# Two fused cross-attention layers: the value products of layer 0 in two sets of head groups, the text keys behind all other key pieces

## What is computed

```
# layer 0
q = heads(x @ Wq.T)
out = softmax(q k_text / 4) v_text + softmax(q k_ip / 4) v_ip
x1 = out @ Wo.T + bo + x
# layer 1: 371 text rows, 4 image rows
probs = softmax(q k / 4);  out = probs v
qsem = l2norm(probs @ text)            # compared with the 4 image rows
p_ip = softmax(q k_ip / 4 + 0.5 * qsem . l2norm(ip)) * mask
y = (out + p_ip v_ip) @ W_out + b_out + x1
```

## Time and profile before

| | before |
|---|---|
| median of 3 runs | 2611.76 us |
| profiled execution, its span | 2613.9 us, 2612.1 us |
| TensorE busy | 2475.8 us, 95% |
| VectorE, ScalarE, GpSimd busy | 1637.9, 1232.6, 767.3 us |
| length of a slot (batch 10: 1178.51 to 1256.80) | 78.3 us |

### The profile page before, as it was taken

The page is one execution under the profiler, slowest core; times in us unless marked ns, Lnnn a source line. Parts: engine busy times, 40 slices in busy tenths (PEclk is TensorE's granted clock), DMA queues, the critical chain, the costliest instruction groups (busy, mean ns, idle before and its releaser), DMA issues.

```text
span 2612.1 us, 64042 instructions
## 1 busy us (share of the span) xinstructions
PE 2475.8 (95%) x26280; PEld 2128.5 (81%) x26280; DVE 1637.9 (63%) x3210; ACT 1232.6 (47%) x2305; POOL 767.3 (29%) x999
## 2 busy tenths in 40 slices
PE   6689999999999999999999999999999999999996
PEld 5578888888888888888888888888888888888874
DVE  2246765666765666776666676566676556677655
ACT  2334445544445544445544445544444544444543
POOL 2123323323323323323322332322322322333222
PEclk7799999999999999999999999999999999999997
DMA  7455777556677555677565777655677655567620
GB/s 181 104 97 87 104 103 93 83 92 92 95 103 91 96 89 86 95 100 107 83 90 86 93 110 101 85 88 86 99 96 104 89 86 89 87 94 101 89 38 7
DMA packets 493225, 241.46 MB, mean 92 GB/s; under 512 B 259627, under 2 KB 492923, under 8 KB 492924
## 3 DMA queue, kind: packets, MB, share of 16 engines
q1 hardware_dynamic: 492934, 237.37, 61.2%
HBM read 171.35 MB, written 64.59 MB: 90 GB/s over the span
## 4 chain that ended last, share of the span: by engine, by line
PE 76%; DVE 17%; issue 2%; SPq 2%; DMA 2%; ACT 1%; POOL 0%; DVEq 0%; ACTq 0%; POOLq 0%
PE ST L690 7%; DVE w L827 6%; PE PN L707 5%; PE R L734 5%; PE R L632 4%; PE R L645 4%; PE R L646 4%; DVE m L911 4%; PE R L583 4%; PE R L584 4%; PE PN L752 3%; PE R L648 3%; PE R L791 3%; PE R L586 3%; DVE w L824 3%; PE ST L672 2%
## 5 line engine op out<-in xcount | busy, mean ns | idle before, releaser
L1126 ACT ACTIVATE p<-ST 128x1344 f32<-128x1344 f32 x320 | 413.6, 1293 | 114.6 <-PE ST L693 110.1
L1256 POOL TENSOR_TENSOR w<-w 128x448 f32<-128x448 f32 (+1 forms) x256 | 330.8, 1292 | 426.3 <-DVE w L824 408.2
L827 DVE SCALAR_TENSOR_TENSOR w<-p,pr 128x1344 f32<-128x1344 f32 x160 | 296.7, 1854 | 174.9 <-ACT pr L1141 161.7
L824 DVE TENSOR_TENSOR rem<-R,kst 128x298 f32<-128x298 f32 (+2 forms) x184 | 91.4, 497 | 455.1 <-ACT kst L1024 455.1
L734 PE MATMUL R<-pr,Gh 128*128 128x448 f32 (+1 forms) x960 | 367.6, 383 | 0.0
L824 DVE TENSOR_TENSOR w<-R,w 128x448 f32<-128x448 f32 (+1 forms) x480 | 281.6, 620 | 71.5 <-PE R L739 61.1
L645 PE MATMUL R<-wvh,ch 128*128 128x320 f32 (+3 forms) x896 | 302.8, 338 | 16.3 <-ACT V0t L1024 12.6
L1189 POOL TENSOR_TENSOR kst<-rem,kst 128x298 bf16<-128x298 f32 (+2 forms) x184 | 151.2, 822 | 483.3 <-ACT kst L1024 262.0
L646 PE MATMUL R<-wvh,cl 128*128 128x320 f32 (+3 forms) x896 | 279.7, 312 | 0.0
L690 PE MATMUL ST<-Qs,Ks 100*128 100x112 bf16 (+1 forms) x3520 | 229.6, 214 | 14.7 <-DMA Qs<-ms 7.6
L690 PEld LDWEIGHTS ST<-Qs,Ks 100*128 100x128 bf16 (+1 forms) x3520 | 184.5, 98 | 67.5 <-issue 35.0
(11 more groups left out here) (185 smaller groups left out, 5834.2 us busy)
## 6 DMA issues: line engine op xcount, KB each, us to landing
Ks<-k_split SPq DMA_DIRECT2D x384, 140.6 KB, 6.1
Ks<-k_split SPq DMA_DIRECT2D x384, 93.8 KB, 8.3
Qs<-q_split SPq DMA_DIRECT2D x384, 70.0 KB, 8.2
w<-in_ctxT SPq DMA_DIRECT2D x31, 750.0 KB, 6.0
k_split<-kst SPq DMA_DIRECT2D x64, 281.2 KB, 3.3
k_split<-kst SPq DMA_DIRECT2D x64, 223.5 KB
q_split<-qst SPq DMA_DIRECT2D x128, 84.0 KB, 2.2
k_split<-kst SPq DMA_DIRECT2D x64, 111.8 KB, 2.5
```

Of the source, the lines that this page charges most:

```text
L824: return e.tensor_tensor(to, x, y, op)
L827: return e.scalar_tensor_tensor(out=to, in0=x, scalar=s, in1=y, op0=op0, op1=op1)
L1126: e.activation(p32[i][:].rearrange("p (u q) -> p u q", u=3), st, ACT.Exp).then_inc(p_whole, 1)
L1256: e.tensor_tensor(first, first, w2[n % 2][0:ROWS[j], QW * j:QW * j + QW], ALU.add).then_inc(ns_added, 1)
```

## The change

In layer 0 the value products no longer follow each group's scores. They are issued in two sets: groups 0, 1 and 2 behind the scores of group 3 and ahead of the piece of that slot place, groups 3 and 4 behind the piece that follows the scores of group 4. To hold five groups of exponentials until then, groups 2 and 3 go to the tiles `w2` (layer 1's, free at that time), group 4 to `p32[0]` again. Groups 0 and 1, and later 3 and 4, lie side by side in bank `PV` and are copied at once; group 2 uses bank `NS`. The transposes now take groups (0, 1), (2) and (3, 4).

The pieces get another order: `k n 0 0`, `q n 0`, `k n 0 1`, `k n None 0`, `k n 1 0`, `k n 1 1`, and behind them the text keys with the text values. The query projection moves from sixth to second, the text keys from fifth to last.

```diff
-PV_PARTS = [((0, 1), (2, 3), (4,)), ((0, 1, 2, 3), (4,))]
+PV_PARTS = [((0, 1), (2,), (3, 4)), ((0, 1, 2, 3), (4,))]
+PV_SETS = ((0, 1, 2), (3, 4))
...
         if n < B:
-            for l, m in ((0, 0), (0, 1), (None, 0), (1, 0)):
+            yield keys(n, 0, 0)
+            yield queries(n, 0)
+            for l, m in ((0, 1), (None, 0), (1, 0), (1, 1)):
                 yield keys(n, l, m)
-            yield text_keys(n), queries(n, 0)
-            yield keys(n, 1, 1)
-            yield text_values(n)
+            yield text_keys(n), text_values(n)
...
     def groups0(b, between):
-        prev = None
+        first = uses[0]
         for g in range(NG + 1):
-            n = scores(b, 0, g) if g < NG else None
+            if g < NG:
+                scores(b, 0, g)
+            if g in (3, 5):
+                which = g // 2 - 1
+                o.add("pv0", b, which, first)
+                o.share("PV", 1, ("pv0", b, which), "pv_read", first + (2, 5)[which])
+                if which == 0:
+                    o.share("NS", 1, ("pv0", b, which), "pv_read", first + 3)
             between(g)
-            if g in (3, 5):
-                turn(b, 0, g // 2 - 1)
-            if g:
-                o.add("pv0", b, g - 1, prev)
-                o.share("PV", 1, ("pv", prev), "pv_read", prev + 1)
-            prev = n
+            if g > 3:
+                turn(b, 0, g - 4)
...
+        def p0_place(g):
+            return (p32[0][:], p32[1][:], w2[0], w2[1], p32[0][:])[g]
+        def pv0_place(g):
+            return ((PV, 0), (PV, 2 * S), (NS, 0), (PV, 0), (PV, 2 * S))[g]
...
+                    for g in PV_SETS[which]:
+                        p, to, c = p0_place(g), *pv0_place(g)
+                        w.wait_ge(p_whole, first + g + 1)
...
-                    if n >= 2:
-                        w.wait_ge(pv_mm, n - 1)
-                        if l_of[n - 2][0] == 1:
-                            w.wait_ge(w_made, l_of[n - 2][1])
+                    if l == 0:
+                        to = p0_place(g)
+                        w.wait_ge(pv_mm, n - 3 if g == 4 else n - g)
...
+                    w.wait_ge(pv_mm, first + (2, 5)[which])
+                    copy(pvt[0][:, 3 * which:3 * which + 2, :],
+                         PV[:, 0:4 * S].rearrange("p (g q) -> p g q", g=2)).then_inc(pv_read, 2)
```

More of the change, by code:

```diff
@@ L695, in tensor @@
                 elif kind == "pv0":
-                    b, g, n = key
-                    p = p32[n % 2]
+                    b, which, first = key
                     w.wait_ge(v_copied, at("v", b, 0, 2))
[L699 to L712, removed]
+                    for g in PV_SETS[which]:
+                        p, to, c = p0_place(g), *pv0_place(g)
+                        w.wait_ge(p_whole, first + g + 1)
+                        if g in (0, 3):
+                            free(w, "PV", ("pv0", b, which))
+                        elif g == 2:
+                            free(w, "NS", ("pv0", b, which))
+                        for u in range(-1, 3):
+                            k = TEXT0 if u < 0 else 119 if u == 2 else 128
+                            for h in range(GH):
+                                hh, q0 = GH * g + h, QW * max(u, 0) + S * h
+                                v, c0 = (V0t[0:k, hh, :], c) if u < 0 else (V0[0:k, u, hh, :], c + S)
+                                if u < 2 or h < GH - 1:
+                                    e.matmul(to[32 * h:32 * h + FV0, c0:c0 + S], v, p[0:k, q0:q0 + S], start=u < 0,
+                                             stop=u == 2, skip_group_check=True)
+                        h = GH - 1
+                        e.matmul(to[32 * h:32 * h + FV0, c + S:c + 2 * S], V0[0:119, 2, GH * g + h, :],
+                                 p[0:119, 2 * QW + S * h:2 * QW + S * h + S], start=False, stop=True,
+                                 skip_group_check=True).then_inc(pv_mm, 1)
@@ L942, in vector @@
                     if l == 0:
-                        c0 = 128 * part
+                        c0 = GH * D * PV_PARTS[0][part][0]
                         if 3 * b + part:
@@ L1118, in scalar @@
                     b, l, g, n = key
-                    i = n % 2
                     st = ST[:, :, 0:QW]
                     w.wait_ge(s_mm, n + 1)
-                    if n >= 2:
-                        w.wait_ge(pv_mm, n - 1)
-                        if l_of[n - 2][0] == 1:
-                            w.wait_ge(w_made, l_of[n - 2][1])
-                    e.activation(p32[i][:].rearrange("p (u q) -> p u q", u=3), st, ACT.Exp).then_inc(p_whole, 1)
-                elif kind in ("pv0", "pv1"):
+                    if l == 0:
+                        to = p0_place(g)
+                        w.wait_ge(pv_mm, n - 3 if g == 4 else n - g)
+                        if b > 1:
+                            w.wait_ge(w_made, NG * (b - 1))
+                        if g in (2, 3):
+                            w.wait_ge(c_low, 4 * min(B, b + 2))
+                            if b > 1:
+                                w.wait_ge(ns_mm, NG * (b - 1))
+                    else:
+                        to = p32[n % 2][:]
+                        w.wait_ge(pv_mm, n - min(g, 1))
+                        if g > 1:
+                            w.wait_ge(w_made, NG * b + g - 1)
@@ new lines, in scalar @@
+                    e.activation(to.rearrange("p (u q) -> p u q", u=3), st, ACT.Exp).then_inc(p_whole, 1)
+                elif kind == "pv0":
+                    b, which, first = key
+                    if b:
+                        w.wait_ge(pvT, at("pvT", b - 1, 0, 2 * which))
+                    w.wait_ge(pv_mm, first + (2, 5)[which])
+                    copy(pvt[0][:, 3 * which:3 * which + 2, :],
+                         PV[:, 0:4 * S].rearrange("p (g q) -> p g q", g=2)).then_inc(pv_read, 2)
+                    if which == 0:
+                        if b:
+                            w.wait_ge(pvT, at("pvT", b - 1, 0, 1))
+                        w.wait_ge(pv_mm, first + 3)
+                        copy(pvt[0][:, 2, :], NS[:, 0:2 * S]).then_inc(pv_read, 1)
+                elif kind == "pv1":
@@ L1128, in scalar @@
                     b, g, n = key
-                    l = int(kind == "pv1")
-                    part = [g in groups for groups in PV_PARTS[l]].index(True)
                     w.wait_ge(pv_mm, n + 1)
                     if b:
-                        w.wait_ge(pvT, at("pvT", b - 1, l, part))
-                    copy(pvt[l][:, g, :], PV[:, 0:(2 - l) * S]).then_inc(pv_read, 1)
+                        w.wait_ge(pvT, at("pvT", b - 1, 1, g // 4))
+                    copy(pvt[1][:, g, :], PV[:, 0:S]).then_inc(pv_read, 1)
@@ L1392, in sync @@
             w.wait_ge(d_out[1], 16 * (B // 2))
-        pv_nth, s_nth, l_of, ready_nth, q_before, m_before = {}, {}, {}, {}, {}, {}
-        firsts, rounds, q_last, m_last = 0, 0, None, None
+        pv_nth, s_nth, ready_nth, q_before, m_before = {}, {}, {}, {}, {}
+        q_last, m_last = None, None
         for kind, key in o.stages:
-            if kind in ("pv0", "pv1"):
+            if kind == "pv0":
+                pv_nth[kind, key[0]] = key[2] + NG
+            elif kind == "pv1":
                 pv_nth[kind, key[0]] = key[2] + 1
@@ L1400, in xattn_two_layers @@
                 s_nth[key[0], key[1], key[2]] = key[3] + 1
-                firsts, rounds = firsts + (key[1] == 0), rounds + (key[1] == 1)
-                l_of[key[3]] = (key[1], firsts if key[1] == 0 else rounds)
             elif kind == "k" and key[1] in (1, None):
```

## The result

| | before | changed |
|---|---|---|
| median of 12 runs each | 2611.57 us (2607.33 to 2612.68) | 2615.15 us (2610.94 to 2621.46) |
| profiled execution, its span | 2613.9, 2612.1 us | 2614.98, 2613.2 us |

The account below looks back on a forecast made before the run. TensorE, busy 95% of the span, was taken as the bound. 2613.9 - 13.2 + 2 + 1 + 8 + 0.5 = 2612.2 us profiled, 2.1 less for the median, stated as 2610.0; 8-in-10 range 2601 to 2618.

Parts of the forecast that it names:

- the start: Slot 0: late query projection and a read-back behind the text keys' write lose 8 us, between 5 and 11.
- My own sign: Slot 1's start: if the forecast is right, it comes 5 to 11 us later than at 164.
- First scores: Slot 0: first scores at 104.9, 5 us later, behind the xT load and a 3.8 us query projection.
- Begin of the read-back: Slot 0: read-back begins at 129.4 instead of 119.18, behind the text keys' write.
- the 2 us that I gave back: Slot 0: the 2.75 us wait at 150.28 shrinks, so maxima 10 us later become 8 us for the start.
- Steady slots: Slots 1 to 30: fewer array-split exits and entries save 0.44 us a slot, 13.2 us; bounds 8.1 to 15.9.
- The query's own 0.03: Steady slots: cost of entering the split from the query projection; the prediction dropped its 0.09 as unshown.
- Rival 3: Steady slots: drains are not saved, only entries gain, 0.17 to 0.26 us a slot; 2616.8 us, chance 0.08.
- The wait for group 2's scores: Steady slots, layer 0: scores wait for ST behind ScalarE's late exponential, 0.13 us in 16 slots, 2 us.
- The bank of the last key piece: Steady slots: the bank is wanted sooner, a wait of 0 to 0.1 us a slot, 1 us in all.
- The last slot: Slot 31, without pieces: set one stands between scores of groups 3 and 4; 0.5 us later.
- Rival 2: Slot 0: idle time puts the first maxima at 1.2 GHz; slot 1 starts 16 us late; 2618.1 us, chance 0.12.

Follow-up runs that it names:

- e3: Changed kernel with xT for batch 1 loaded at the program's start, ahead of the first maxima; 2611.63 us, ratio 0.9997 to the kernel before.
- e2: Changed kernel with slot 0's read-back of keys and queries issued ahead of the text keys' write; 2611.83 us, ratio 0.9996 to the kernel before.
- e4: Changed kernel with the edits of e2 and e3 together; 2606.28 us against 2612.95 for the kernel before, ratio 0.9975.
- second pair: Changed kernel and kernel before, both unchanged, profiled again; spans 2615.4 and 2606.1 us; the changed kernel's new median 2615.05 us, ratio 1.0012.
- e1: Changed kernel with the old order of pieces in slot 0 alone; 2608.85 us against 2612.95 for the kernel before, ratio 0.9983.
- e7: Changed kernel with ScalarE making a key's middle part behind the next exponential instead of ahead; 2616.62 us, ratio 1.0010 to the kernel before.
- e6: Changed kernel with the new piece order but value products group by group as before; 2626.61 us (6 runs), ratio 1.0050 to the kernel before.
- e8: Changed kernel with the edits of e4 and e7 together; 2610.15 us against 2614.59 for the kernel before, ratio 0.9981.
- e5: Changed kernel with the two sets but the old order of pieces in all slots; 2619.30 us against 2614.59 for the kernel before, ratio 1.0023.

## Why the prediction was wrong

**The step that failed** is the first slot's: "I take 8 us for the start, between 5 and 11". It is 12 us (10.2 by the first pair of profiles, 13.8 by the second), above my upper end on average. The direction hangs on it: with 8 in its place the three terms give 8 + 2.4 - 11.5, 1.1 us less than before, and with 12.0 they give 2.9 more. My own sign, slot 1 starting 5 to 11 us later, came out as 11.5 and 17.1. The mechanism was the forecast one, and e3, e2 and e4 show its two parts: a late load and a late read-back, on one chain. By its links, measured from the transpose of slot 0's maxima, first pair:

- First scores: 5.6 us later, forecast 5. The projection took 3.97 us from its start to the scores (102.69 to 106.66), forecast 3.8. It ran at half clock, and that this costs so much was right: the clock is 0.50 from 102.70 to 106.60, and it was 0.50 from 90 to 95 too, so the wait of 6.76 us did not bring it. The page TensorE: Matmul & The Clock Gate of the Trainium skill, in Part 1, has the throttled state as the default; the 0.50 at the start agrees.
- Begin of the read-back: 10.9 later, forecast 10.2; in the second pair 12.8, since that profile of before came to it earlier.
- From its start to the first maxima: 18.7 us (18.55 in the second profile), where I kept the 17.2 of before. It is 17.2 and 17.5 in the two profiles of before and 18.0 to 19.4 in e1 to e7; e6 has 18.7 without sets and e8 17.1 with them, so the sets alone do not decide it. It goes with the time to issue the six query transfers: 5.3 to 5.6 us in before and e8, 6.35 in e2, 6.9 to 7.2 in the others. Why that varies was not found.
- From the maxima to slot 1: 25.9 us, before 28.1, which is the 2 us that I gave back. But in the second profile of before it is 25.4, and then nothing is given back: the wait of 2.75 us is 1.33 there, and the clock, 0.57 from 151 to 156 in the first profile, is 1.00.

```profile
148.75 0.50 PE L672 MATMUL ST<-Ks,Qs 96*112 96x375 bf16 x2 [1.33 <-issue]
```

I had taken one execution's wait for a property of the kernel. Of the term, then, the 10 us to the read-back were nearly right; the 1.0 to 1.5 us more of the read-back had been put at nothing, and the 2 us given back are not there in the second pair.

**Steady slots.** Forecast, net: 13.2 less 2 less 1, so 10.2 us; measured 11.1 and 11.9. The drains behaved as worked out: with the waits of 2.6 us and the drops added back, the gain is some 0.5 us a slot (e5 gives 14 us over the slots in the same way, though its waits ate them), forecast 0.44. Two terms account for a part of the surplus. A group inside a set costs 0.77, not the 0.80 of layer 1's products. The query's own 0.03 was dropped. The page TensorEngine Tiling (Array Packing) of the Trainium skill, Key Properties, has each change of the tiling mode drain the engine; the measured 0.12 for leaving, and 0.70 against 0.59 for entering from scores, agree, while for the query projection 0.03 is left of it. Rival 3, that no drains are saved, is refuted by the 2.43 for three groups.

**What is late next.** The wait for group 2's scores: 16 slots by 0.16, 2.6 us, forecast 16 by 0.13. The bank of the last key piece: 0.5 us in the first profile and nothing in the second, forecast 1. Both hold.

**The last slot.** Forecast 0.5; 0.7 in the first pair, 4.1 in the second, 2.4 on average. Over all twelve profiles the stretch takes 119.4 to 122.0 us in the nine with sets and 116.8 to 118.7 in the three without, 3 us apart in the mean, so this term too was mis-sized. TensorE's rows there, answering to the earlier trace rows:

```profile
2498.10 1.21 PE L702 MATMUL ST<-Qs,Ks 102*128 102x112 bf16 x11 [1.38 <-ACT p L1151]
...
2500.78 1.21 PE L702 MATMUL ST<-Qs,Ks 102*128 102x112 bf16 x11 [1.38 <-ACT w L1151]
...
2502.01 0.58 PE L723 MATMUL PN<-p,V0t 77*17 77x112 f32 x8
```

Four exponentials now follow each other with nothing but scores between, TensorE stands idle three times (1.28, 1.38 and 1.38 us; before 1.28, 0.49 and 0.49), and the scores take 1.21 instead of 0.67 to 0.72. The window behind shows the first set at the low clock in both profiles of the changed kernel, and the same work at full clock in both of before; the first profile of each:

```profile
2500.00:2505.00 5.00, 4.22 (x100) 3.90 (x104) 0.00 (x0) 2.20 (x3) 0.00 (x0) 0.61 0.01 1
```

```profile
2500.00:2505.00 5.00, 4.22 (x100) 3.28 (x101) 0.97 (x3) 3.19 (x4) 0.00 (x0) 1.00 0.01 3
```

I had priced the order there, and not what the idle time does to the clock.

**The chances.** Rival 2 (16 us at the start) was as near to the measured 12 as the forecast's 8, and got 0.12 against 0.55; but its mechanism, a whole first stretch of maxima at the low clock and later work shifted with it, did not come: the clock is 0.50 for 5 us behind the wait, and from the maxima to slot 1 it takes 25.9 us, less than the 28.1 of before. The difference to before, 3.6 us, is under the 5.2 that I called indistinguishable; with 12 runs each the interval tells it from none. The steady term and the start's term were each known to about 3 us and nearly cancel, so the sign was not to be had from them; the 0.18 for slower was too little beside 0.27 for faster.

## What to carry to other kernels

Joining products that share an array split is worth the drains (here 0.5 us a slot) only where the exponentials have time between the scores: count the engine that frees the scores' bank first. When an order of work is changed for the steady state, write the first and the last round's order by itself: there a load's place in the queue and a write ahead of a read-back cost 10 us (e4), nearly what 30 rounds gained. And read a start from two profiles at least, since a wait and a stretch at low clock in one may be gone in the next.

## What the hardware showed that I had not expected

The granted clock falls to half for a few microseconds in the middle of a busy kernel. In TensorE's timeline of the changed kernel, slot 3:

```profile
388.65 0.50 PE L684 MATMUL ST<-Ks,Qs 96*112 96x375 bf16 x2 [0.62 <-DVE m L927]
...
390.26 0.37 PE L684 MATMUL PN<-Ks,Qs 96*112 96x375 bf16 x1 [0.55 <-DVE m L927]
...
391.82 0.47 PE L657 MATMUL R<-wvh,ch 128*128 128x320 f32 x1
392.09 0.47 PE L658 MATMUL R<-wvh,cl 128*128 128x320 f32 x1
```

Behind two waits of 0.62 and 0.55 us the value projections (L657) come every 0.27 us instead of every 0.15, for 3.4 us, and the slot is 2.1 us longer. The wait of the first kind stands in nine places of this trace between slots 1 and 31, and the clock falls behind two of them; in the kernel before, seven and one. Over the twelve profiles each of the nine slots that are 2 us long has such a wait, of 0.61 to 0.71 us; but waits of that length stand in other slots too (0.62 us in slot 13 of this trace) and their slots are not 2 us longer. What decides it stays open. The price is some 2.1 us each, none to three in an execution, which is of the size of the differences between these kernels.
